# Layer 0's attention with its scores, exponentials and reciprocals one unit further ahead of the transposes, on four score buffers in place of three

## The chip, the cores and the metric

One core of one Trainium2 chip. The metric is the device time of one launch in microseconds, median of several executions. TensorE (PE) multiplies and transposes, VectorE (DVE) and ScalarE (ACT) read its results out of PSUM, GpSimd (POOL) works on SBUF only, and SyncE starts most of the loads. Each engine works through its own queue in order; semaphores order them against each other.

## The reference, cut to what matters

Four attention layers in a row, each with its projections and its MLP or norm. The change touches layer 0 alone, whose attention is

```python
# x: context (4, 64, 256); latents: (4, 256, 256); NH = 16 heads of DH = 16
h = jnp.concatenate([x, latents], axis=1)
q = (latents @ q_w + q_b).reshape(b, k_len, NH, DH)
kv = (h @ kv_w + kv_b).reshape(b, p + k_len, NH, DH, 2)
kmat, v = (kv[..., 0], kv[..., 1])
attn = jnp.einsum('bkhd,bnhd->bhkn', q, kmat) / DH
attn = jnp.where(full_mask[:, None, None, :], attn, -jnp.inf)
attn = jax.nn.softmax(attn.astype(jnp.float32), axis=-1).astype(q.dtype)
attn_out = jnp.einsum('bhkn,bnhd->bkhd', attn, v)  # then out_w, out_b, residual, rmsnorm, MLP
```

So for each of 4 batches and 16 heads there are 256 queries against 320 keys (256 latents, 64 of the context, the latter masked).

## The kernel before, in words

Layer 0's attention is cut into 64 units, 16 for each batch. A unit is one block of 128 queries and one pair of heads (`units0`, L299), so two score matrices of 128 x 320. Each unit passes through these stations:

- TensorE makes the scores (`scores0`, L568, matmul at L577) into a wide PSUM slot. Of three wide slots, two (`SCORES`) are for scores and one (`TURNS`) for transposes. A slot is taken again when it has been drained (`Ring`, `take_wide`); the scores of unit u therefore wait for the exponentials of unit u-2.
- VectorE (`front0`, L1277) adds the mask to 64 of the columns (L1282), takes the maxima (L1286) and multiplies them by -1/16 (L1287).
- ScalarE (`exp0`, L964) takes the exponentials out of PSUM into the SBUF tile `scoresb`, one instruction for each head with its row sum in `sums` (L970).
- VectorE (`middle0`, L1289) takes the reciprocal of the sums (L1291).
- GpSimd (`normalize0`, L1507) multiplies by it into `probs`, in two instructions (L1514) of 128x512 and 128x128. `probs` has two buffers, so it first waits until TensorE has turned unit u-2.
- TensorE (`turn_probs`, L474) transposes `probs` in five 128x128 pieces (L479) into the one wide slot for transposes.
- ScalarE (`probs_turned`, L937, copy at L897) copies them to SBUF, which frees that slot.
- After each fourth unit TensorE multiplies four transposed units with the values (`values0`, L581, L599).

The order in each queue is written out by hand as a loop over steps; step s is the one in which unit s is transposed. TensorE's step s is: transposes of unit s, scores of unit s+3, the value products if s is a multiple of 4, then one side product. ScalarE's is: the copy of the side product of step s-1, the copy of the transposes of s, the exponentials of s+2. VectorE's is: `front0` of s+2, `middle0` of s+1, its share of the side copy of step s-1, and at some steps more. GpSimd's step s is: the multiply of unit s, then a bias addition (steps 4 to 19).

The side products (`SIDE0`, `side_product0`) are the projections of queries, keys and values for the next batch, their placement into operands for the score products (`qhot` L554, `kpair` L564), and the output projection of the batch before (`proj`, L512). They share one narrow PSUM slot with their copies. The last batch has none of the next batch's. The side products of batch 0 are made ahead of the loop: `START0[0]` before the first scores, `START0[1]` at step -1, before that step's scores.

Two more things hang on the steps. At two steps of each later batch (18 and 19 of batch 1 and so on, `done0`) VectorE makes the statistics of a row block, GpSimd raises them to the power -1/2 (L1478) at the end of its step, and VectorE scales. At steps 22 and 38 VectorE splits weights of the MLP (`weights_low`, L224: a subtraction with both inputs in SBUF), and ScalarE copies them at steps 20 and 36 (L218).

The rings of `scoresb`, `mx`, `sums` and `rcp` have three buffers, taken by u % 3. `exp0` waits until GpSimd has multiplied unit u-3 out of its buffer.

Of the kernel before, what the change touches and what calls it, by code (L numbers as in the profile page):

```python
# [20 lines left out]
P = 128  # L21
B, S, D, T = 4, 256, 256, 64
# [7 lines left out]
KEYS0 = S + T  # L30
# [7 lines left out]
ALU = mybir.AluOpType  # L38
# [68 lines left out]
def build(nc, t, out):  # L107
    ctx = ExitStack()
    with ctx:
# [219 lines left out]
        def side0(step):  # L329
# [8 lines left out]
                return (job, b) if 0 < b < B else (None, None)  # L338
            return (job, b + 1) if b + 1 < B else (None, None)

        TURNED0 = 6

        def turned_probs(u):
# [31 lines left out]
        def _(pe):  # L375
# [229 lines left out]
            for job in START0[0]:  # L605
                side_product0(job, 0, (0, 1))
            n0 = len(units0)
            for step in range(-3, n0 + 3):
                if step == -1:
                    for job in START0[1]:  # L610
                        side_product0(job, 0, (0, 1))
                if 0 <= step < n0:
                    turn_probs(step)
                if step + 3 < n0:
                    scores0(step + 3)
                if step > 0 and step % 4 == 0:
# [273 lines left out]
        def _(act):  # L890
# [73 lines left out]
            def exp0(u):  # L964
                key = ("S", u)
                act.wait_ge(max_ready, u + 1)
                if u >= 3:
                    act.wait_ge(prob_ready, probcount[u - 2])
                for i in range(2):
                    nc.scalar.activation(scoresb[:, u % 3, i * KEYS0:(i + 1) * KEYS0],  # L970
                                         wide_ps[:, wide.slot(key), i * 512:i * 512 + KEYS0], ACT.Exp,
                                         scale=1.0 / 16, bias=mx[:, u % 3, i:i + 1],
                                         accum_out=sums[:, u % 3, i:i + 1]).then_inc(wide.drained[wide.slot(key)], 1)

            def exp(u, n):
                if n == 1024:
# [25 lines left out]
            for job in START0[0]:  # L1002
                side0_copy(job, 0)
            n0 = len(units0)
            for step in range(-2, n0 + 2):
                if step == 0:
                    for job in START0[1]:
                        side0_copy(job, 0)
                job, b = side0(step - 1)
                if job:  # L1010
                    side0_copy(job, b)
                if step - 2 >= 0 and (step - 2) % 8 == 7:
                    b, c = (step - 2) // 16, (step - 2) // 8 % 2
# [110 lines left out]
        def _(dve):  # L1124
# [152 lines left out]
            def front0(u):  # L1277
                b, r, q = units0[u]
                key = ("S", u)
                dve.wait_ge(*wide.full(key))  # L1280
                ps = wide_ps[:, wide.slot(key), :].rearrange("p (i n) -> p i n", i=2)
                link(v.tensor_tensor(ps[:, :, S:KEYS0], ps[:, :, S:KEYS0],  # L1282
                                     mask0[:, b, :].unsqueeze(1).broadcast_to([P, 2, T]), ALU.add))
                if u >= 3:
                    dve.wait_ge(*wide.empty(("S", u - 3)))
                link(v.tensor_reduce(mx[:, u % 3, 4:6], ps[:, :, 0:KEYS0], AX, ALU.max))  # L1286
                v.tensor_scalar(mx[:, u % 3, 0:2], mx[:, u % 3, 4:6], -1.0 / 16, None, ALU.mult).then_inc(max_ready, 1)  # L1287

            def middle0(u):  # L1289
                dve.wait_ge(*wide.empty(("S", u)))  # L1290
                v.reciprocal(rcp[:, u % 3, 0:2], sums[:, u % 3, 0:2]).then_inc(rcp_ready, 1)  # L1291

            dve.wait_ge(load["cols"], 16)
            for job in START0[0]:
# [1 line left out]
            dve.wait_ge(load["mask0"], 16)  # L1296
            link(v.tensor_scalar(mask0[:].rearrange("p b k -> p (b k)"), mask0i, 0, NEG0, ALU.is_equal, ALU.mult))
            n0 = len(units0)
            for step in range(-2, n0 + 5):
                if step == 0:  # L1300
                    for job in START0[1]:
                        side0_copy(job, 0)
                if step + 2 < n0:
                    front0(step + 2)
                if 0 <= step + 1 < n0:
                    middle0(step + 1)
                job, b = side0(step - 1)
                if job:
                    side0_copy(job, b)
# [146 lines left out]
        def _(pool):  # L1456
# [50 lines left out]
            def normalize0(u):  # L1507
                pool.wait_ge(rcp_ready, u + 1)
                if u >= 2:
                    pool.wait_ge(*wide.full(("T", u - 2)))  # L1510
                s3 = scoresb[:, u % 3, 0:2 * KEYS0].rearrange("p (i k) -> p i k", i=2)
                for lo, hi, o in ((0, S, 0), (S, KEYS0, 2 * S)):
                    n = hi - lo
                    g.tensor_tensor(probs[:, u % 2, o:o + 2 * n].rearrange("p (i k) -> p i k", i=2), s3[:, :, lo:hi],  # L1514
                                    rcp[:, u % 3, 0:2].unsqueeze(2).broadcast_to([P, 2, n]), ALU.mult).then_inc(prob_ready, 1)

            def spread_keys(layer, kbd, mask, heads_):
                pool.wait_ge(*wide.empty(("k", layer)))
# [102 lines left out]
```

## Time and profile before

| what | value |
|---|---|
| median of 3 runs | 840.12 us (840.08 to 841.82) |
| the profiled execution's own time | 840.74 us |
| its span, first to last instruction | 839.0 us |
| instructions | 12837 |
| busy: TensorE, VectorE, ScalarE, GpSimd | 730.8, 532.9, 403.9, 360.2 us |
| mean granted TensorE clock | 0.937 |
| first and last transposes of layer 0 | 25.70 and 199.30 us |

The profile lists each instruction with its start and length in microseconds from the start of the span. "x5" says how many instructions a line merges; the bracket at its end gives the idle time of the engine before it and the instruction whose completion ended that. A clock of 1.00 is TensorE's full 2.4 GHz, 0.50 the lower level of 1.2 GHz.

### The profile page before, as it was taken

What the parts mean: (1) busy time and instruction counts of PE and PEld (TensorE: products, weight loads), DVE (VectorE), ACT (ScalarE), POOL (GpSimd) and SP (SyncE); (2) the same over time, 40 slices, a digit from 0 to 9 for tenths busy, and PEclk for the clock granted to TensorE, in tenths of its full rate; (3) what the DMA queues carried; (4) which work ended last, traced back from release to release, by engine and by line L of the source; (5) the groups of instructions that cost most, each with busy time, mean ns of one, the idle gap of its engine ahead of it and who ended that gap; (6) DMA issues with size and microseconds to landing.
All of it is one profiled execution on the core that took longest, in us unless ns stands there. A gap on an engine that the chain in (4) does not pass through costs nothing.

```text
span 839.0 us, 12837 instructions
## 1 busy us (share of the span) xinstructions
PE 730.8 (87%) x4752; PEld 556.6 (66%) x4752; DVE 532.9 (64%) x1034; ACT 403.9 (48%) x965; POOL 360.2 (43%) x383
## 2 busy tenths in 40 slices
PE   8888888876399888779999999999998799776798
PEld 6676666654289445557875787876677688344598
DVE  6577776753844599955537674433888557398644
ACT  3687878854231377645652233653242131376421
POOL 2487554543700488844315561000765502177200
PEclk9899999967699999989999999999999899996899
DMA  8200000000000600002432000332000000200000
GB/s 318 95 1 1 2 1 2 2 1 2 0 1 1 201 1 2 1 1 92 161 103 98 1 1 1 101 104 97 1 0 1 1 1 1 100 1 1 1 20 32
DMA packets 24957, 32.51 MB, mean 39 GB/s; under 512 B 2752, under 2 KB 19392, under 8 KB 24768
## 3 DMA queue, kind: packets, MB, share of 16 engines
q1 hardware_dynamic: 24336, 31.10, 10.9%
q8 instruction: 39, 0.64, 0.3%
q10 hardware_dynamic: 560, 0.59, 0.2%
q14 instruction: 22, 0.18, 0.1%
HBM read 30.64 MB, written 1.05 MB: 38 GB/s over the span
## 4 chain that ended last, share of the span: by engine, by line
PE 62%; DVE 18%; POOL 8%; issue 7%; ACT 4%; DMA 1%; SPq 0%; POOLq 0%; DVEq 0%
PE wide_ps L432 9%; PE narrow_ps L451 8%; PE wide_ps L741 7%; PE wide_ps L692 6%; PE wide_ps L479 5%; PE narrow_ps L776 5%; POOL probs L1514 4%; PE wide_ps L715 4%; PE wide_ps L728 4%; DVE scoresb L1207 2%; DVE mx L1216 2%; PE narrow_ps L599 2%; DVE sums L1223 2%; PE wide_ps L412 2%; POOL probs L1500 2%
## 5 line engine op out<-in xcount | busy, mean ns | idle before, releaser
L479 PE MATMUL wide_ps<-ident,probs 128*128 128x128 f32 x640 | 96.3, 291 | 49.0 <-POOL probs L1500 23.1
L1492 POOL TENSOR_TENSOR scoresb<-scoresb,mx 128x768 f32<-128x768 f32 (+1 forms) x40 | 70.7, 1767 | 153.0 <-DVE mx L1214 115.4
L479 PEld LDWEIGHTS wide_ps<-ident,probs 128*128 128x128 f32 x640 | 77.2, 150 | 79.2 <-issue 63.2
L1514 POOL TENSOR_TENSOR probs<-scoresb,rcp 128x512 f32<-128x512 f32 (+1 forms) x128 | 89.4, 720 | 71.3 <-DVE rcp L1291 70.1
L897 ACT ACTIVATE probsT<-wide_ps 128x1024 f32<-128x1024 f32 (+1 forms) x73 | 64.3, 881 | 114.9 <-PE wide_ps L479 114.7
L1478 POOL TENSOR_TENSOR rstd<-veps,mhalf 128x1 f32<-128x1 f32 x56 | 32.0, 572 | 136.1 <-DVE veps L1142 136.1
L1500 POOL TENSOR_TENSOR probs<-scoresb,rcp 128x1024 f32<-128x1024 f32 x40 | 78.2, 1954 | 7.6 <-DVE rcp L1224 7.6
L432 PE MATMUL wide_ps<-xq_r,wstream_r 128*128 128x512 f32 x192 | 65.3, 424 | 8.7 <-issue 6.9
L451 PEld LDWEIGHTS narrow_ps<-wstream_r,hidden 128*128 128x128 f32 x576 | 69.2, 188 | 1.2 <-DVE xB L1170 0.5
L451 PE MATMUL narrow_ps<-wstream_r,hidden 128*128 128x256 f32 x576 | 69.7, 281 | 0.3 <-DVE xB L1170 0.3
L970 ACT ACTIVATE scoresb<-wide_ps,mx 128x320 f32<-128x320 f32 x128 | 66.4, 531 | 1.9 <-DVE mx L1287 1.6
L692 PE MATMUL wide_ps<-scoresb_r,probs_r 128*128 128x256 f32 x256 | 57.1, 306 | 4.8 <-DVE vwb L1370 4.2
L933 ACT ACTIVATE scoresb<-wide_ps,col 128x512 f32<-128x512 f32 x48 | 30.4, 685 | 63.0 <-PE wide_ps L432 63.0
L776 PE MATMUL narrow_ps<-region,probsT 128*128 128x256 f32 x256 | 58.0, 380 | 1.4 <-DVE xB L1170 1.4
L741 PE MATMUL wide_ps<-region,actT 128*128 128x512 f32 x128 | 59.0, 602 | 0.0
L1286 DVE TENSOR_REDUCE mx<-wide_ps 128x2 f32<-128x640 f32 x64 | 52.8, 824 | 2.3
L1323 DVE TENSOR_TENSOR wstream_r<-wstream,probs_r 128x256 fp32r<-128x256 f32 x64 | 26.7, 462 | 41.1 <-ACT probs_r L1059 41.1
L776 PEld LDWEIGHTS narrow_ps<-region,probsT 128*128 128x128 f32 x256 | 47.8, 191 | 7.5 <-DVE xB L1170 1.6
L692 PEld LDWEIGHTS wide_ps<-scoresb_r,probs_r 128*128 128x128 f32 x256 | 43.2, 196 | 12.4 <-issue 6.8
L432 PEld LDWEIGHTS wide_ps<-xq_r,wstream_r 128*128 128x128 f32 x192 | 38.9, 206 | 18.9 <-issue 7.5
L432 PE MATMUL wide_ps<-actT_r,wstream_r 128*128 128x512 f32 x96 | 41.1, 428 | 11.0 <-DVE actT_r L1184 11.0
L1170 DVE TENSOR_TENSOR xB<-narrow_ps,xB 128x256 f32<-128x256 f32 x48 | 20.2, 420 | 46.0 <-PE narrow_ps L451 24.1
(163 smaller groups left out, 1625.5 us busy)
## 6 DMA issues: line engine op xcount, KB each, us to landing
wstream<-in_L_xattn_wk SPq DMA_DIRECT2D x8, 512.0 KB, 4.0
wstream<-in_L_xattn_wv SPq DMA_DIRECT2D x8, 512.0 KB, 5.2
wstream<-in_L_xattn_wo SPq DMA_DIRECT2D x8, 512.0 KB, 6.4
wstream<-in_wqT SPq DMA_DIRECT2D x8, 512.0 KB, 7.5
wstream<-in_L_xattn_mlp_w SPq DMA_DIRECT2D x2, 1024.0 KB, 10.7
wstream<-in_L_xattn_w_fc SPq DMA_DIRECT2D x2, 1024.0 KB, 6.2
rows<-in_rows SPq DMA_DIRECT2D x1, 1280.0 KB, 14.0
xq<-in_x SPq DMA_DIRECT2D x1, 1024.0 KB, 11.8
```

The costliest lines, as they stand in the source:

```text
L432: m = mm(ps[:, j * 512:(j + 1) * 512], w1[pw][:, kc, f * P:(f + 1) * P], xparts[px][:, kc, half * 512:(half + 1) * 512], start=kc == 0 and ...
L451: m = mm(ps[:, 0:D], hidden[:, ph, f, qoff((q + i) % 4)], w2[pw][:, f, :], start=f == 0 and part == 0, stop=f == NF - 1 and part == 2)
L479: m = nc.tensor.transpose(ps[:, j * P:(j + 1) * P], probs[:, u % 2, j * P:(j + 1) * P], ident[:])
L692: last = mm(ps[:, m * 256:(m + 1) * 256], w[:, m, kc, :], cparts[:, part, kc, :], start=kc == 0 and i == 0, stop=kc == NC - 1 and i == 2)
L741: m = mm(ps[:, g * 512:(g + 1) * 512], actT[:, c, qoff(q)], G[:, c, 8 * g:8 * g + 8, b * T:(b + 1) * T], start=c == 0, stop=c == NC - 1)
L776: mm(ps[:, 0:D], probsT[:, u % 2, r * P:(r + 1) * P], VW[:, q // 2, r, :], start=r == 0, stop=False)
L897: nc.scalar.activation(dst, src, ACT.Identity, **kw).then_inc(ring.drained[ring.slot(key)], 1)
L970: nc.scalar.activation(scoresb[:, u % 3, i * KEYS0:(i + 1) * KEYS0], wide_ps[:, wide.slot(key), i * 512:i * 512 + KEYS0], ACT.Exp, scale=1 ...
L1286: link(v.tensor_reduce(mx[:, u % 3, 4:6], ps[:, :, 0:KEYS0], AX, ALU.max))
L1492: g.tensor_tensor(s3[:, first:], s3[:, first:], mx[:, u % 3, first:].unsqueeze(2).broadcast_to([P, 16 - first, n_scores]), ALU.subtract).t ...
L1500: g.tensor_tensor(probs[:, u % 2, :].rearrange("p (h k) -> p h k", h=16), s3[:, :, 0:T], rcp[:, u % 3, :].unsqueeze(2).broadcast_to([P, 16 ...
L1514: g.tensor_tensor(probs[:, u % 2, o:o + 2 * n].rearrange("p (i k) -> p i k", i=2), s3[:, :, lo:hi], rcp[:, u % 3, 0:2].unsqueeze(2).broadc ...
```

## The change

The loops of layer 0 begin one step earlier, and TensorE's scores, VectorE's `front0` and `middle0` and ScalarE's `exp0` stand one unit further ahead of the step. The multiply, the transposes, their copy, the values and all side work keep their step. The four rings of small and large buffers have four places. They lie in the same tiles, which are addressed flat: a unit's scores take 640 of the 3120 columns of `scoresb`, its maxima, sums and reciprocals 8 of 48 columns.

```diff
+        RING0, AHEAD0 = 4, 3
+
+        def scores_of(u):
+
+            return scoresb[:].rearrange("p a n -> p (a n)")[:, u % RING0 * 2 * KEYS0:(u % RING0 + 1) * 2 * KEYS0]
+
+        def pair_of(tile, u, o=0):
+
+            o += u % RING0 * 8
+            return tile[:].rearrange("p a n -> p (a n)")[:, o:o + 2]
...
-            for step in range(-3, n0 + 3):
+            for step in range(-1 - AHEAD0, n0 + 3):
                 if step == -1:
                     for job in START0[1]:
                         side_product0(job, 0, (0, 1))
                 if 0 <= step < n0:
                     turn_probs(step)
-                if step + 3 < n0:
-                    scores0(step + 3)
+                if step + 1 + AHEAD0 < n0:
+                    scores0(step + 1 + AHEAD0)
...
                 act.wait_ge(max_ready, u + 1)
-                if u >= 3:
-                    act.wait_ge(prob_ready, probcount[u - 2])
+                if u >= RING0:
+                    act.wait_ge(prob_ready, probcount[u - RING0 + 1])
...
-            for step in range(-2, n0 + 2):
+            for step in range(-AHEAD0, n0 + 2):
...
-                if step + 2 < n0:
-                    exp0(step + 2)
+                if step + AHEAD0 < n0:
+                    exp0(step + AHEAD0)
...
-                if u >= 3:
-                    dve.wait_ge(*wide.empty(("S", u - 3)))
+                if u >= RING0:
+                    dve.wait_ge(*wide.empty(("S", u - RING0)))
...
-            for step in range(-2, n0 + 5):
+            for step in range(-AHEAD0, n0 + 5):
                 if step == 0:
                     for job in START0[1]:
                         side0_copy(job, 0)
-                if step + 2 < n0:
-                    front0(step + 2)
-                if 0 <= step + 1 < n0:
-                    middle0(step + 1)
+                if step + AHEAD0 < n0:
+                    front0(step + AHEAD0)
+                if 0 <= step + AHEAD0 - 1 < n0:
+                    middle0(step + AHEAD0 - 1)
```

Every `[:, u % 3, ...]` of `exp0`, `front0`, `middle0` and `normalize0` becomes `scores_of(u)` or `pair_of(tile, u)`.

## Rows read from the trace of the kernel before

**Rows 1.** Busy time in the last batch: window, length, engines, PEclk, DMA share, GB/s

```profile
158.61:200.04 41.43, 28.84 (x276) 21.84 (x276) 22.86 (x68) 26.64 (x78) 21.98 (x32) 0.84 0.00 1
```

**Rows 2.** Waits from 25 to 206 us: total, times, longest

```profile
PE wide_ps L479 <- POOL probs L1514: 21.8, 20, 2.6
```

**Rows 3.** Timeline from 186 to 191 us: start, length, engine, line

```profile
187.13 0.70 ACT L897 ACTIVATE turned<-wide_ps 128x640 f32<-128x640 f32 x1 [0.23 <-PE wide_ps L479]
...
187.73 0.52 ACT L970 ACTIVATE scoresb<-wide_ps,mx 128x320 f32<-128x320 f32 x1
...
188.64 0.21 ACT L970 ACTIVATION_READ_ACCUMULATOR scoresb<-wide_ps,mx 128x1 f32 x1
188.74 0.71 ACT L897 ACTIVATE turned<-wide_ps 128x640 f32<-128x640 f32 x1
...
189.13 1.40 POOL L1514 TENSOR_TENSOR probs<-scoresb,rcp 128x512 f32<-128x512 f32 x2 [2.13 <-DVE rcp L1291]
...
189.84 0.82 DVE L1286 TENSOR_REDUCE mx<-wide_ps 128x2 f32<-128x640 f32 x1
```

**Rows 4.** TensorE's timeline of the last batch, its transposes alone

```profile
177.26 0.77 PE L479 MATMUL wide_ps<-ident,probs 128*128 128x128 f32 x5 [0.50 <-ACT turned L897]
...
180.04 1.30 PE L479 MATMUL wide_ps<-ident,probs 128*128 128x128 f32 x5 [1.21 <-POOL probs L1514]
...
186.28 0.81 PE L479 MATMUL wide_ps<-ident,probs 128*128 128x128 f32 x5
...
190.67 0.74 PE L479 MATMUL wide_ps<-ident,probs 128*128 128x128 f32 x5 [1.21 <-POOL probs L1514]
...
192.55 0.74 PE L479 MATMUL wide_ps<-ident,probs 128*128 128x128 f32 x5 [0.85 <-POOL probs L1514]
...
194.99 0.74 PE L479 MATMUL wide_ps<-ident,probs 128*128 128x128 f32 x5
...
199.30 0.74 PE L479 MATMUL wide_ps<-ident,probs 128*128 128x128 f32 x5 [1.70 <-POOL probs L1514]
```

**Rows 5.** Timeline around a row norm in the last batch

```profile
165.59 0.55 POOL L1478 TENSOR_TENSOR rstd<-veps,mhalf 128x1 f32<-128x1 f32 x1 [2.65 <-DVE veps L1142]
...
167.64 0.74 PE L479 MATMUL wide_ps<-ident,probs 128*128 128x128 f32 x5 [2.07 <-POOL probs L1514]
```

**Rows 6.** The chain that ended last, two value groups: start, length, what

```profile
59.39 1.23 PE narrow_ps L599 x40
...
184.06 2.29 PE narrow_ps L599 x40
```

**Rows 7.** Busy time from 180 to 187 us, columns as in rows 1

```profile
180.00:187.00 7.00, 6.69 (x60) 5.39 (x61) 2.98 (x11) 3.92 (x11) 4.19 (x6) 0.54 0.01 2
```

**Rows 8.** A dense stretch: busy time as in rows 1, and one wait of TensorE

```profile
81.00:119.00 38.00, 32.89 (x337) 26.84 (x336) 27.06 (x72) 33.47 (x90) 19.29 (x28) 1.00 0.01 2
...
93.04 0.74 PE L479 MATMUL wide_ps<-ident,probs 128*128 128x128 f32 x5 [0.23 <-POOL probs L1514]
```

**Rows 9.** The start: timeline of TensorE and ScalarE from 12 to 37 us

```profile
14.81 1.90 PE L535 MATMUL narrow_ps<-wstream,actT 128*128 128x256 f32 x8
...
17.22 0.20 ACT L970 ACTIVATION_READ_ACCUMULATOR scoresb<-wide_ps,mx 128x1 f32 x1
...
25.70 0.71 PE L479 MATMUL wide_ps<-ident,probs 128*128 128x128 f32 x5
...
33.46 1.30 PE L479 MATMUL wide_ps<-ident,probs 128*128 128x128 f32 x5 [0.91 <-POOL probs L1514]
```

**Rows 10.** Scaling of maxima (min/median/max ns, and one of them), transposes and a weight split

```profile
L1287 DVE TENSOR_SCALAR mx<-mx x64: 169/170/566, 16.1 to 195.0; 128x2 f32<-128x2 f32 x64
...
166.61 0.56 DVE L1287 TENSOR_SCALAR mx<-mx 128x2 f32<-128x2 f32 x1
...
87.21 0.71 PE L479 MATMUL wide_ps<-ident,probs 128*128 128x128 f32 x5
...
88.86 1.22 DVE L224 TENSOR_TENSOR wstream_r<-wstream,wstream_r 128x1024 fp32r<-128x1024 f32 x1
```

More of the change, by code:

```diff
@@ L966, in exp0 @@
                 act.wait_ge(max_ready, u + 1)
-                if u >= 3:
-                    act.wait_ge(prob_ready, probcount[u - 2])
+                if u >= RING0:
+                    act.wait_ge(prob_ready, probcount[u - RING0 + 1])
                 for i in range(2):
-                    nc.scalar.activation(scoresb[:, u % 3, i * KEYS0:(i + 1) * KEYS0],
+                    nc.scalar.activation(scores_of(u)[:, i * KEYS0:(i + 1) * KEYS0],
                                          wide_ps[:, wide.slot(key), i * 512:i * 512 + KEYS0], ACT.Exp,
-                                         scale=1.0 / 16, bias=mx[:, u % 3, i:i + 1],
-                                         accum_out=sums[:, u % 3, i:i + 1]).then_inc(wide.drained[wide.slot(key)], 1)
+                                         scale=1.0 / 16, bias=pair_of(mx, u)[:, i:i + 1],
+                                         accum_out=pair_of(sums, u)[:, i:i + 1]).then_inc(wide.drained[wide.slot(key)], 1)
             def exp(u, n):
@@ L1283, in front0 @@
                                      mask0[:, b, :].unsqueeze(1).broadcast_to([P, 2, T]), ALU.add))
-                if u >= 3:
-                    dve.wait_ge(*wide.empty(("S", u - 3)))
-                link(v.tensor_reduce(mx[:, u % 3, 4:6], ps[:, :, 0:KEYS0], AX, ALU.max))
-                v.tensor_scalar(mx[:, u % 3, 0:2], mx[:, u % 3, 4:6], -1.0 / 16, None, ALU.mult).then_inc(max_ready, 1)
+                if u >= RING0:
+                    dve.wait_ge(*wide.empty(("S", u - RING0)))
+                link(v.tensor_reduce(pair_of(mx, u, 4), ps[:, :, 0:KEYS0], AX, ALU.max))
+                v.tensor_scalar(pair_of(mx, u), pair_of(mx, u, 4), -1.0 / 16, None, ALU.mult).then_inc(max_ready, 1)
             def middle0(u):
                 dve.wait_ge(*wide.empty(("S", u)))
-                v.reciprocal(rcp[:, u % 3, 0:2], sums[:, u % 3, 0:2]).then_inc(rcp_ready, 1)
+                v.reciprocal(pair_of(rcp, u), pair_of(sums, u)).then_inc(rcp_ready, 1)
             dve.wait_ge(load["cols"], 16)
@@ L1510, in normalize0 @@
                     pool.wait_ge(*wide.full(("T", u - 2)))
-                s3 = scoresb[:, u % 3, 0:2 * KEYS0].rearrange("p (i k) -> p i k", i=2)
+                s3 = scores_of(u).rearrange("p (i k) -> p i k", i=2)
                 for lo, hi, o in ((0, S, 0), (S, KEYS0, 2 * S)):
@@ L1514, in normalize0 @@
                     g.tensor_tensor(probs[:, u % 2, o:o + 2 * n].rearrange("p (i k) -> p i k", i=2), s3[:, :, lo:hi],
-                                    rcp[:, u % 3, 0:2].unsqueeze(2).broadcast_to([P, 2, n]), ALU.mult).then_inc(prob_ready, 1)
+                                    pair_of(rcp, u).unsqueeze(2).broadcast_to([P, 2, n]), ALU.mult).then_inc(prob_ready, 1)
             def spread_keys(layer, kbd, mask, heads_):
```

## The prediction, made before the changed kernel was run

> **What bounds layer 0 now.** I began with the busy time by batch. The last of the four batches (units 48 to 63) has almost no side products left and still takes 41.43 us, while no engine is busy in it for more than 28.84 [rows 1]. So it waits. The totals of waits say for what: 20 times in layer 0 a group of transposes found TensorE idle until GpSimd's multiply was done, 21.8 us together [rows 2].
>
> Then one ring, followed event by event in the last batch. The transposes of unit 57 begin at 186.28 [rows 4]. ScalarE copies them at 187.13, its next exponentials (unit 59) end at 188.64 + 0.21 = 188.85, VectorE's reciprocal releases GpSimd, which multiplies from 189.13 for 1.40 [rows 3], and TensorE turns unit 59 at 190.67 [rows 4]. The ring spans two units because exponentials run two ahead: 190.67 - 186.28 = 4.39, or 2.19 us a unit. Nothing faster is open while the multiply is in it.
>
> **Which rings the change opens.** Counted by the step of the transposes, nothing but the multiply moves. Before, at step s, ScalarE exponentiates unit s+2, VectorE reduces s+2 and inverts s+1; after, s+3, s+3 and s+2. TensorE makes scores s+3 before and s+4 after, into the same two score slots, so they still wait for exponentials made one step earlier. Side copies, row statistics and weight splits keep their step. Only this differs: the reciprocal at VectorE's step s now serves the transposes of s+2 instead of s+1. The ring above then holds three units, 4.39 / 3 = 1.46 a unit, and is no longer the longest.
>
> Late next are two rings. ScalarE alone: copy at 187.13, next copy at 188.74, 1.61 a unit [rows 3]. The two score slots: exponentials end at 188.85, the maximum behind them runs 189.84 + 0.82 = 190.66, its scaling about 0.2, exponentials 188.85 - 187.73 = 1.12: 192.0, or 3.13 for two units, 1.57 each [rows 3]. I take 1.65, the 1.61 with a few hundredths lost between the two.
>
> **The last batch.** Up to unit 54 I change nothing: the transposes at 167.64 waited 2.07 us for a multiply that stood in GpSimd's queue behind a row-norm power, which waited for statistics that VectorE makes at the same step as before [rows 5]. From unit 54 to 63 the turns run from 177.26 to 199.30, 22.04 us for nine steps [rows 4]. Two of them also carry the value products (after units 56 and 60). Seven plain steps: 7 x 1.65 = 11.55. The value step with scores took 194.99 - 192.55 = 2.44 at full clock [rows 4]; the second has no scores left in it, about 0.5 less, 1.9; ScalarE's copy of attended values adds some 0.2 to each. 2.44 + 1.9 + 0.4 = 4.74. Sum 16.3, so **5.7 us saved**. This counts both value groups at full clock. Before, the one at 184.06 took 2.29 us against 1.23 for the same 40 matmuls at 59.39 [rows 6], because the granted clock averaged 0.54 of full (nearly all at the lower level, 1.2 GHz) from 180 to 187 [rows 7], right after TensorE sat idle for 1.21 before 180.04 [rows 4]. That idle time goes, so I take the full clock; at the lower level 1.06 less is saved.
>
> **The dense batches.** From 81 to 119 ScalarE is busy 33.47 of 38.00 us; most waits for the multiply are hidden under its queue there. What shows is a wait of 0.23 at the transposes of unit 24 [rows 8], with a fellow in each neighbouring batch: 3 x 0.23 = **0.7 saved**. The bound above is all of ScalarE's idle time, 4.5 here and some 13.6 in the three dense stretches; the bound below is nothing. I stay near the bottom because side products and their copies keep their step and end the other waits.
>
> **The lead-in, which pays.** Scores of unit 2 are now made before the opening side products, and their slot is free only when unit 0's exponentials end, 17.22 + 0.20 = 17.42; the side products started at 14.81 [rows 9]. TensorE's in-order queue holds all of the opening products behind that wait: with some 0.3 for the two score products, 2.9 late, and so the first transposes, 28.6 for 25.70 [rows 9]. VectorE reduces unit 2 ahead of its opening copies, but those wait for the late products anyway. Then it is won back, for unit 1's multiply is already done at 28.6. Following the slots (0.7 copy, 1.12 exponentials, 1.4 mask to maximum, 1.4 multiply) I get transposes of units 0 to 3 at 28.6, 30.2, 32.2 and 33.9, the last where 33.46 stood [rows 9]. **0.4 lost**; between 0 and 2.9.
>
> **GpSimd against VectorE.** The 2-element scaling of maxima takes 0.17 in the median and up to 0.57; one of 0.56 began at 166.61, during the first half (1.05 long) of the multiply that followed the power at 165.59, and ended with it [rows 5, 10]. So two such instructions exclude one another. The multiply of unit u, early now, waits for the transposes of unit u-2: unit 24's starts at 87.21 + 0.71 = 87.92 and runs to 89.3, across the weight split that VectorE starts at 88.86 [rows 10]; unit 40's meets the second split likewise. No row shows a split held, so I bound it: 0 to 1.4 each (the pair's length); 0.5 taken, the 0.44 of that overlap being the nearest, **1.0 lost** in two. Elsewhere the scaling has slack before ScalarE needs its result.
>
> The Trainium skill (SBUF — State Buffer, Who interferes with whom) states a rule: a VectorE instruction with two SBUF inputs and a GpSimd instruction that reads SBUF exclude each other for the whole instruction. By it the splits are held some 0.4 and 0.9, 1.3 where I took 1.0; no row here shows a split held.
>
> The addressing edits (a ring of four in the same tiles) change no shape or count: the same instructions, no DMA moved, SyncE untouched. The work after unit 63 and the later layers shift whole.
>
> **Sum.** -5.7 - 0.7 + 0.4 + 1.0 = -5.0. The profiled execution took 840.74 (span 839.0), so 835.7 by it; the median of the runs is 0.62 lower, 840.12, so **835.1**. A measurement can tell about 0.2%, 1.7 us, from no change.
>
> **Rivals.**
> (a) The lower clock stays in the last batch: one group of values 1.06 longer, two transposes 0.5 together: 836.7. For it: from 167 to 173 TensorE still idles behind row norms. 0.15.
> (b) The dense batches gain too: two fifths of the 13.6 idle comes back, 5.5 more, 829.6. Against: ScalarE's queue is nearly full, and what it waits for there are side products. 0.12.
> (c) Two score slots set the pace, and running ahead gives only storage; lead-in and splits alone count, 840.1 + 1.4 = 841.5, or 840 where they are hidden. Against it: their ring of 1.57 is shorter than 2.19. 0.08.
> (d) Slower: the multiply, held until the transposes two back, slides over VectorE's scaling in every unit and holds maxima, exponentials and side copies by 0.57 - 0.17 = 0.40. It decides from 5.0 + 1.7 = 6.7 lost, 17 units on the path; with 23 of the 64 the time is 844.3. For it: the rows of the scaling. Against: few units have VectorE on the path. 0.05.
> The forecast has 0.60.
>
> **Range and chances.** Low end: (b), 829.5. High end: (a) with 1.2 lost in the lead-in and 2.0 in the splits, 838.5, rounded up to 839.0. Faster by over 0.2%: forecast, (a) and (b), 0.87; within: (c), 0.08; slower: (d), 0.05.
>
> **What would show it.** Turns of units 54 to 63 near 1.65 apart where 2.19 stood; the multiply hardly named among the waits of transposes, but for the row norms, whose 2 us waits stay; first transposes near 28.6; the value groups of the last batch near 1.23; the two splits over 1.22. Wrong would be: scaling rows of 0.5 all over with ScalarE waiting on VectorE, or last turns still over 2 us apart while each multiply ended long before.

## The result and the profile after

| | before | after |
|---|---|---|
| median of the runs in this comparison | 840.45 us (4 runs, 840.08 to 841.82) | 828.71 us (4 runs, 827.73 to 831.71) |
| the profiled execution, its span | 840.74, 839.0 us | 827.73, 826.0 us |
| mean granted TensorE clock | 0.937 | 0.957 |
| first and last transposes of layer 0 | 25.70, 199.30 us | 28.53, 193.69 us |

The ratio is 0.9863, interval 0.9836 to 0.9891: 11.7 us less, where 5.0 was forecast, and 828.7 lies just under the low end of the range, 829.5. The profiled execution after is the fastest of its four, so the two profiles lie 13.0 apart. A kernel is now and then executed in a slower state with a lower clock; one run below was (840.49, experiment 2), and its ratio leaves it out. Lines of the kernel after are those of before plus 11 (transposes L490, their copy L908, exponentials L981, scaling of maxima L1298, multiply L1525, scores L588).

The page of the kernel after: its busy times, and the transposes (busy time and mean ns of one, then the idle time before them; all four layers).

```profile
PE 719.2 (87%) x4752; PEld 544.8 (66%) x4752; DVE 537.8 (65%) x1034; ACT 403.6 (49%) x965; POOL 362.3 (44%) x383
...
L490 PE MATMUL wide_ps<-ident,probs 128*128 128x128 f32 x640 | 93.4, 285 | 39.1 <-POOL probs L1511 24.0
```

The same 4752 matmuls are busy for 11.6 us less than before (730.8): already a sign of the clock, since the change takes none away.

The totals of waits from 25 to 200 us, and a transposition behind a row norm in the last batch, kernel after.

```profile
PE wide_ps L490 <- POOL probs L1525: 9.2, 5, 2.1
```

```profile
168.87 0.94 PE L490 MATMUL wide_ps<-ident,probs 128*128 128x128 f32 x5 [2.08 <-POOL probs L1525]
```

Twenty waits for the multiply, 21.8 us [rows 2], have become five. All five stand at or behind row norms; the first behind each norm is as long as it was, 2.08 beside 2.07 [rows 5].

The timeline of the kernel after in the last batch: transposes of units 54, 56, 57 and 63, and some events behind unit 58's.

```profile
177.90 0.77 PE L490 MATMUL wide_ps<-ident,probs 128*128 128x128 f32 x5 [0.50 <-ACT turned L908]
...
181.13 0.77 PE L490 MATMUL wide_ps<-ident,probs 128*128 128x128 f32 x5
...
183.87 0.76 PE L490 MATMUL wide_ps<-ident,probs 128*128 128x128 f32 x5
...
186.27 0.71 ACT L908 ACTIVATE turned<-wide_ps 128x640 f32<-128x640 f32 x1
...
186.44 0.56 PE L588 MATMUL wide_ps<-kpair,qhot 128*128 128x320 f32 x2 [0.25 <-ACT scoresb L981]
...
186.66 1.40 POOL L1525 TENSOR_TENSOR probs<-scoresb,rcp 128x512 f32<-128x512 f32 x2 [0.49 <-DVE rcp L1302]
...
187.86 0.73 ACT L908 ACTIVATE turned<-wide_ps 128x640 f32<-128x640 f32 x1
...
193.69 0.77 PE L490 MATMUL wide_ps<-ident,probs 128*128 128x128 f32 x5 [0.80 <-ACT probsT L908]
```

Plain steps (those without value products) are 1.55 to 1.62 long, ScalarE's two copies stand 1.59 apart without idle time between them, and TensorE's waits now name ScalarE. Units 54 to 63 take 193.69 - 177.90 = 15.79 for 22.04 [rows 4].

**Where the 13.0 us between the two profiles came from.** Stages are cut at the starts of instructions, the same ones in each kernel; this table, worked out from those starts, is used for the experiments too.

| stage, from the end of the one before up to | before | after |
|---|---|---|
| last transposes of layer 0 | 199.30 | 193.69 |
| "exit": first projection of the last batch (before L512) | 4.58 | 3.55 |
| "entry": first low product of the MLP (L432 with `actT_r`) | 23.92 | 21.72 |
| first scores of layer 1 | 57.15 | 58.03 |
| "preparation": first head product of layer 2 (L715) | 91.95 | 89.94 |
| first scores of layer 2 (L741) | 62.10 | 62.19 |
| last head product | 137.35 | 135.68 |
| last scores of layer 2 | 48.67 | 48.67 |
| "last stretch": last product of the last MLP (L451) | 211.17 | 209.70 |

In this pair layer 0 gave 5.6, the exit 1.0, the entry 2.2, preparation 2.0, the head products 1.7, the last stretch 1.5, and 1.0 went back in between. So over half of the gain lies behind unit 63, in code that is the same in both.

How far a single pair can be trusted, the profiles of the experiments tell. Layer 0 of before is in two of them (199.30, and 195.42 in experiment 6), that of after in five (190.86 to 193.69, experiments 5, 8, 9 and 10 among them), so its share is 5 us in the mean, and 5.6 is one draw. Behind unit 63 up to the last product, before and experiments 1 and 6 (less its delay) took 636.9 to 639.6, after and experiments 2 and 4 took 629.5 to 632.3: 6.7 in the mean for the 7.4 of this pair. Exit and entry repeat to 0.05 us wherever nothing in them was edited. The head products (135.7 to 138.3) and the last stretch (208.1 to 213.8) do not, and no experiment here ties their 1.7 and 1.5 to the change.

Busy time by windows at the exit and in the preparation (its ends rounded), of before and then of after (columns as in rows 1: length, PE, PEld, DVE, ACT, POOL, granted clock).

```profile
199.30:203.88 4.58, 3.10 (x45) 2.31 (x46) 0.00 (x0) 1.18 (x2) 0.00 (x0) 0.58 0.02 4
285.00:376.90 91.90, 72.42 (x515) 43.59 (x514) 77.95 (x146) 57.04 (x183) 62.55 (x46) 0.93 0.03 11
```

```profile
193.69:197.24 3.55, 2.07 (x46) 1.59 (x46) 0.00 (x0) 1.18 (x2) 0.00 (x0) 1.00 0.02 5
277.00:366.90 89.90, 69.70 (x514) 41.60 (x514) 77.84 (x146) 57.19 (x183) 61.42 (x45) 0.96 0.04 12
```

The counts match but for one instruction here and there, VectorE's and ScalarE's busy times within 0.3%; TensorE's time and its clock differ. At the exit the clock is 0.58 against 1.00, and all of the 1.03 us is TensorE's: 3.10 busy against 2.07.

The timeline from the projections to the first low product, of before and then of after.

```profile
203.88 2.05 PE L512 MATMUL narrow_ps<-wstream,xq 128*128 128x256 f32 x4 [0.69 <-ACT xq L897]
...
208.32 2.88 PE L494 MATMUL wide_ps<-ctxT,wkrep 128*128 128x256 f32 x8
...
212.15 14.51 POOL L1520 TENSOR_TENSOR region<-headbuf,head 128x4096 f32<-128x4096 f32 x2 [1.42 <-ACT headbuf L897]
...
213.40 6.35 DVE L1182 CAST xq_r<-actT 128x1024 fp32r<-128x1024 f32 x1 [2.28 <-ACT actT L897]
...
219.79 7.96 DVE L1184 TENSOR_TENSOR actT_r<-actT,xq_r 128x1024 fp32r<-128x1024 f32 x1
...
227.80 0.80 PE L432 MATMUL wide_ps<-actT_r,wstream_r 128*128 128x512 f32 x1 [6.75 <-DVE actT_r L1184]
```

```profile
197.24 1.10 PE L523 MATMUL narrow_ps<-wstream,xq 128*128 128x256 f32 x4 [0.69 <-ACT xq L908]
...
199.82 1.89 PE L505 MATMUL wide_ps<-ctxT,wkrep 128*128 128x256 f32 x8
...
202.99 14.11 POOL L1531 TENSOR_TENSOR region<-headbuf,head 128x4096 f32<-128x4096 f32 x2
...
203.06 7.13 DVE L1159 TENSOR_SCALAR xn<-xB,rstd 128x256 f32<-128x256 f32 x1 [0.66 <-POOL rstd L1489]
...
210.11 7.54 DVE L1193 CAST xq_r<-actT 128x1024 fp32r<-128x1024 f32 x1
...
218.96 0.80 PE L443 MATMUL wide_ps<-actT_r,wstream_r 128*128 128x512 f32 x1
```

Read it by GpSimd. It spreads layer 1's keys (`spread_keys`) in two instructions of some 7 us, as soon as ScalarE has copied the keys out of PSUM, and VectorE's work on the MLP's input stands still meanwhile. In both kernels the first low product follows the start of the spreading by nearly the same time: 227.80 - 212.15 = 15.65 and 218.96 - 202.99 = 15.97. Spreading begins 8.27 us behind the first projection before, and 5.75 after, since projections and keys run at the full clock, 1.10 for 2.05 and 1.89 for 2.88. That is the 2.2 of the entry.

### The profile page after: what moved, and what is told of

Same layout as the page of the kernel before. It is cut to its first block, busy times and chain, and to the rows that moved or that the text cites. A ratio compares the mean times of both kernels' runs of the same rounds, so it can differ in the third digit from the quotient of the medians.

```text
span 826.0 us, 12835 instructions
## 1 busy us (share of the span) xinstructions
PE 719.2 (87%) x4752; PEld 544.8 (66%) x4752; DVE 537.8 (65%) x1034; ACT 403.6 (49%) x965; POOL 362.3 (44%) x383
## 4 chain that ended last, share of the span: by engine, by line
PE 62%; DVE 17%; ACT 8%; issue 6%; POOL 6%; DMA 1%; SPq 0%; DVEq 0%; POOLq 0%
PE wide_ps L443 9%; PE narrow_ps L462 8%; PE wide_ps L752 7%; PE wide_ps L703 5%; PE narrow_ps L787 5%; PE wide_ps L490 4%; PE wide_ps L739 4%; PE wide_ps L726 3%; ACT scoresb L981 3%; DVE scoresb L1218 2%; PE narrow_ps L610 2%; DVE mx L1227 2%; POOL probs L1511 2%; DVE sums L1234 2%; PE wide_ps L423 2%
## 5 line engine op out<-in xcount | busy, mean ns | idle before, releaser
L490 PE MATMUL wide_ps<-ident,probs 128*128 128x128 f32 x640 | 93.4, 285 | 39.1 <-POOL probs L1511 24.0
L490 PEld LDWEIGHTS wide_ps<-ident,probs 128*128 128x128 f32 x640 | 74.2, 146 | 68.1 <-issue 58.4
L908 ACT ACTIVATE probsT<-wide_ps 128x1024 f32<-128x1024 f32 (+1 forms) x73 | 64.5, 883 | 110.6 <-PE wide_ps L490 110.2
L1525 POOL TENSOR_TENSOR probs<-scoresb,rcp 128x512 f32<-128x512 f32 (+1 forms) x128 | 91.5, 738 | 56.9 <-DVE rcp L1302 29.4
L981 ACT ACTIVATE scoresb<-wide_ps,mx 128x320 f32<-128x320 f32 x128 | 66.8, 537 | 3.8 <-DVE mx L1298 3.5
L703 PE MATMUL wide_ps<-scoresb_r,probs_r 128*128 128x256 f32 x256 | 54.7, 297 | 5.3 <-DVE vwb L1381 4.2
L703 PEld LDWEIGHTS wide_ps<-scoresb_r,probs_r 128*128 128x128 f32 x256 | 41.4, 188 | 13.1 <-issue 7.5
```

Of the source, the lines that this page charges most:

```text
L490: m = nc.tensor.transpose(ps[:, j * P:(j + 1) * P], probs[:, u % 2, j * P:(j + 1) * P], ident[:])
L703: last = mm(ps[:, m * 256:(m + 1) * 256], w[:, m, kc, :], cparts[:, part, kc, :], start=kc == 0 and i == 0, stop=kc == NC - 1 and i == 2)
L908: nc.scalar.activation(dst, src, ACT.Identity, **kw).then_inc(ring.drained[ring.slot(key)], 1)
L981: nc.scalar.activation(scores_of(u)[:, i * KEYS0:(i + 1) * KEYS0], wide_ps[:, wide.slot(key), i * 512:i * 512 + KEYS0], ACT.Exp, scale=1.0 ...
```

## Theories

**T1**, the forecast's: distance takes the multiply out of the ring (the cycle of events that spans two units), and everything behind unit 63 shifts whole; storage alone does nothing. **T2**: buffers give the gain. **T3**, formed on the table above: TensorE waits less at the end of layer 0, so its clock stays up through the exit, and what follows is shortened by that. **T3'**, rival to it: what follows depends on when it comes, not on the clock.

## Experiments

Ratios are against runs of the kernel before on the same chip (its median there 840.2 to 840.3), so medians of different experiments can be set beside one another to about a microsecond. A stage's length is from one profiled execution.

**1. Four buffers, old distance** (kernel after with one line changed).

```diff
-        RING0, AHEAD0 = 4, 3
+        RING0, AHEAD0 = 4, 2
```

> The changed kernel with its four buffers, but scores, maxima, exponentials and reciprocals back at their old distance (two units ahead). Theory 'ring': all of the gain comes from taking the multiply out of the two-unit ring, so buffers alone give nothing: 840.4, last transposes of layer 0 near 199.3 us. Theory 'buffers': the fourth buffer relieves a wait of its own (the exponentials' for the multiply three units back): then under 838.

837.63 us, ratio 0.9976 (0.9956 to 0.9995). The profiled execution was the slowest of ten, 841.48. Its transposes of units 59 and 60:

```profile
188.68 0.74 PE L490 MATMUL wide_ps<-ident,probs 128*128 128x128 f32 x5 [1.21 <-POOL probs L1525]
190.56 0.74 PE L490 MATMUL wide_ps<-ident,probs 128*128 128x128 f32 x5 [0.84 <-POOL probs L1525]
```

The old waits, 1.21 and 0.84 where 1.21 and 0.85 stood [rows 4]; units 54 to 63 take 21.44, 0.6 less than before. 837.63 is just under the 838 that was named as the sign of T2, so T1's "storage alone does nothing" isn't exact either: a quarter of a per cent comes from the buffers, and the rest of the gain doesn't.

**2. Three buffers, new distance.**

```diff
-        RING0, AHEAD0 = 4, 3
+        RING0, AHEAD0 = 3, 3
```

> The changed kernel with three buffers again and the distance of three units kept. Exponentials of unit s+3 stand behind the copy of the transposes of unit s, which already needs unit s multiplied, so theory 'ring' says that the third buffer is free in time and the fourth not needed: 828.7, within 1.5. Theory 'buffers': the exponentials wait for the multiply and the time goes back towards 835 to 840.

830.22 us over all four runs, 828.28 in the profiled one, 0.9877 (0.9836 to 0.9919); units 54 to 63 take 15.78. The distance is the change; at that distance the fourth buffer can't be told from no fourth buffer.

**3. Four ahead.**

```diff
-        RING0, AHEAD0 = 4, 3
+        RING0, AHEAD0 = 4, 4
```

> The changed kernel with the distance raised once more, to four units. The ring through the multiply is then 4.3 / 4 = 1.1 us a unit; at three units (1.46) it was already shorter than ScalarE's own 1.61. Theory 'ring': the pace of the last batch stays at 1.55 to 1.62 a unit and the extra scores ahead of the opening products cost one more microsecond or so of lead-in: turns of units 54 to 63 spaced as with the change, total 828 to 830.5. If the pace were still set by the distance, the last batch shrinks again: under 826.

833.93 us, 0.9922 (0.99 to 0.9944), over the 828 to 830.5 expected. Plain steps stay at 1.56 to 1.62: with the multiply out of the ring, more distance finds nothing. The two value steps are longer, 3.30 and 2.17, so units 54 to 63 take 16.60. And it costs a second wait ahead of the opening products (TensorE's timeline):

```profile
17.35 0.56 PE L588 MATMUL wide_ps<-kpair,qhot 128*128 128x320 f32 x2 [2.48 <-ACT scoresb L981]
18.61 0.90 PE L588 MATMUL wide_ps<-kpair,qhot 128*128 128x320 f32 x2 [0.71 <-ACT scoresb L981]
19.31 3.13 PE L546 MATMUL narrow_ps<-wstream,actT 128*128 128x256 f32 x8
```

The opening products, 1.90 long before [rows 9], take 3.13 here, and unit 0 is turned at 31.25 (28.53 after), unit 4 at 42.36 (36.66). Preparation, 92.9 for 89.9, adds to the loss.

**4. Opening products ahead of the third unit's scores** (kernel after; the same edit in ScalarE's and VectorE's loops, from step 0 to -1).

```diff
-                if step == -1:
+                if step == -2:
                     for job in START0[1]:
                         side_product0(job, 0, (0, 1))
```

> The changed kernel with the opening side products (START0[1]) and their copies one step earlier on TensorE, ScalarE and VectorE, so ahead of the scores of unit 2. The prediction's lead-in step says that the first transposes come back from 28.5 to about 25.7, and that most of this is given back at once, because unit 1 is then inverted behind the opening copies: transposes of unit 4 at 36.0 to 36.7 (36.66 with the change), total 828 to 829. The rival, that the late start is carried through, says 825.9.

827.28 us, 0.9846 (0.9815 to 0.9876), against 828.71 no certain difference, and between the 828 to 829 expected and the 825.9 of the rival. Unit 0 is turned at 26.80 for 28.53, but unit 4 at 36.23 for 36.66: of the 1.7 gained at unit 0, 0.4 is left four units on, since the kernel after wins most of its late start back by itself. Between unit 0 and unit 4 it takes 8.1 us in each of the five profiles with this layer 0, where this kernel takes 9.4. The 25.70 of before isn't reached: the third unit's scores stand behind the opening products, ahead of unit 0's transposes.

**5. A delay at the exit.** Eight linked copies of the identity (each waits for the one before it) into a tile of their own on ScalarE, ahead of the last copy of attended values; extra work, never read. In the kernel after:

```diff
+                    if step - 2 == n0 - 1:
+                        for i in range(8):
+                            nc.scalar.copy(idle[:], ident[:].unsqueeze(1).broadcast_to([P, 2, P])).then_inc(idled, 1)
+                            act.wait_ge(idled, i + 1)
```

> The changed kernel with eight idle copies (128x256, linked one behind the other) on ScalarE ahead of the last copy of attended values of layer 0, some 3 us between layer 0's attention and everything behind it. Theory 'rigid' (the later layers' time doesn't depend on when they start): 828.7 + 3.0 to 3.5, that is 831.7 to 832.2. Theory 'phase' (the extra gain after layer 0 is where the low clock level happens to fall): another amount by over 1.5 us, most likely up, 834 to 837.

835.69 us, 0.996 (0.9933 to 0.9987). A delay of 3.48 cost 7.0 by the medians, 8.1 by the ratios. The timeline of that kernel:

```profile
194.00 3.46 ACT L1031 COPY idle<-ident 128x256 f32<-128x256 f32 x8 [1.42 <-PE narrow_ps L612]
...
198.10 2.05 PE L525 MATMUL narrow_ps<-wstream,xq 128*128 128x256 f32 x4 [4.17 <-ACT xq L910]
...
202.54 2.79 PE L507 MATMUL wide_ps<-ctxT,wkrep 128*128 128x256 f32 x8
...
221.92 0.79 PE L445 MATMUL wide_ps<-actT_r,wstream_r 128*128 128x512 f32 x1 [6.75 <-DVE actT_r L1201]
```

After 4.17 us without work TensorE's projection takes 2.05 again and the keys 2.79, and the stages are those of before: entry 23.82, then 57.11, preparation 92.0. From the last transposes to the first head product of layer 2 it is 179.92 against 173.23: 6.7 of the 7.0, of which the delay itself is half.

**6. The same delay in the kernel before.**

> The kernel before with the same eight idle copies on ScalarE ahead of the last attended values (3.5 us in the run with the change). Theory 'phase in two modes': after layer 0 the changed kernel runs its exit and the layer 2 preparation in a quick mode (exit from projection to first MLP product 21.7 us, preparation 89.9) and the kernel before, and the changed one when delayed, in a slow mode (23.8 and 92.0). The kernel before is in the slow mode already, so a delay costs only itself: 840.2 + 3.5 = 843.7, stages 23.8 and 92.0. Theory 'each shift is a new draw': 840 to 847, with other stage lengths.

844.63 us, 1.0051 (1.0031 to 1.007): 4.4 for 3.5. Its profiled execution was the fastest of ten, 840.42, with exit 4.58 + 3.48 = 8.06, and entry 23.94, then 57.16 and preparation 91.9, unchanged. There the delay had nothing more to spoil. This speaks for T3. Its profile also gives a warning: its layer 0, the very instructions of before, ended at 195.42 instead of 199.30. Much of the 3.9 us is the clock: it is 0.92 against 1.00 from 60 to 81 us, and unit 41 is turned 4.55 behind unit 40 in the one (the clock 0.76 from 138 to 145), 2.95 in the other. Differences of up to 4 us in layer 0 between two single profiles prove nothing.

**7. TensorE kept busy in the kernel before.** Four transposes of the identity into unused columns of PSUM ahead of the transposes of units 55, 59, 62 and 63 (while TensorE waits for the multiply), ahead of the last group of values and of the first projection of the last batch; extra work, never read.

```diff
+            def keep_warm(ps, o):
+                for i in range(4):
+                    nc.tensor.transpose(ps[:, o:o + P], ident[:], ident[:])
...
+                if u in (55, 59, 62, 63):
+                    keep_warm(ps, 768)
```

> The kernel before, with 24 transposes of the identity (results never read) put into TensorE's waits for the multiply at units 55, 59, 62 and 63 and into its two waits of layer 0's exit. They fill idle time, so by themselves they cost nothing. If the changed kernel's gain behind unit 63 comes from TensorE being at full clock there, this one gets it without the change: value group of units 52 to 55 at 1.23 in place of 2.29, last transposes near 198 (199.3 less 1.1), exit 3.55 + 21.7 in place of 4.58 + 23.9, preparation 89.9, total 833.5 to 835. If the gain comes from something else: 838 to 841.

835.87 us, 0.9935 (0.9912 to 0.9958), a little over the 833.5 to 835 expected. TensorE's windows and its timeline in that kernel:

```profile
180.00:187.00 7.00, 4.82 (x64) 3.69 (x64) 4.84 (x14) 6.35 (x18) 4.50 (x7) 1.00 0.01 2
196.11:199.66 3.55, 3.10 (x54) 2.45 (x54) 0.00 (x0) 1.18 (x2) 0.00 (x0) 1.00 0.02 5
279.20:372.00 92.80, 73.84 (x514) 44.25 (x513) 78.04 (x146) 57.04 (x183) 62.54 (x46) 0.91 0.04 12
```

```profile
198.90 0.66 PE L386 MATMUL narrow_ps<-ident 128*128 128x128 f32 x4
199.66 1.10 PE L520 MATMUL narrow_ps<-wstream,xq 128*128 128x256 f32 x4
...
202.24 1.89 PE L500 MATMUL wide_ps<-ctxT,wkrep 128*128 128x256 f32 x8
```

The clock from 180 to 187 is 1.00 for 0.54 [rows 7], the exit 3.55 and the entry 21.71, the very lengths of the kernel after, with nothing of layer 0's distance changed: extra matmuls put into waits took 4.4 us off, of which units 54 to 63 are 2.2 (19.82 for 22.04). So exit and entry are shown to hang on the clock, in both directions: 4.58 and 23.9 in all profiles with the old distance and no extra transposes (before, experiments 1 and 6, less the delay), 3.55 in all with the new and no delay, and 21.7 wherever the spreading of keys was left alone too. The preparation took 92.8, not 89.9: T3 does not reach that far by itself.

**8. Spreading held until VectorE has the normed rows** (kernel after, GpSimd).

```diff
+            pool.wait_ge(xn_ready, NQ)
             spread_keys(1, kbd1, head8, 16)
```

> The changed kernel with GpSimd's spreading of layer 1's keys (two instructions of 7.05 us) waiting for the last row norm. In both traces the first MLP product that needs a split input starts 15.65 to 16.0 us behind the start of the spreading, because VectorE's casts and subtractions stand still during it. If the spreading holds VectorE, the last norm (7.13 us in the changed kernel, 0.35 before) takes 0.35 again, the spreading starts about 0.5 later, and the product too: nothing gained, 829 to 829.5. If the 7.13 us of the norm were on the path by themselves, the product comes 6.8 us earlier: 822.

831.37 us, 0.9866 (0.9827 to 0.9905), where 829 to 829.5 was expected if nothing is gained and 822 if the norm counted; entry 21.89. The norm's 7.13 is gone, and the next two instructions of VectorE take 7.16 and 7.96 in its place: who is held doesn't matter, that someone is held for the length of the spreading does.

**9. Spreading held until the MLP's input is split.**

```diff
+            pool.wait_ge(x_split, 4)
             spread_keys(1, kbd1, head8, 16)
```

> The changed kernel with the spreading waiting until VectorE has split the MLP's input. If the spreading holds VectorE, the norm, casts and subtractions take 0.35, 0.69 and 1.23 again and the first low product starts near 206.5 instead of 218.96; the two 7 us blocks then fall into the MLP, where VectorE splits the hidden layer each 2.8 us and TensorE stalls for part of them: total 820 to 826. If VectorE's long instructions are long for another reason, nothing changes: 828.7.

826.81 us, 0.9858 (0.9801 to 0.9915), over the 820 to 826 expected; one of its four runs took 836.75, and there is no certain difference from 828.71. The first low product comes at 205.84, an entry of 8.69 for 21.72, but 8.3 is given back by layer 1's first scores (66.38 for 58.03), since the spreading now holds the weight splits and the casts of `hidden` (timeline):

```profile
207.57 9.23 DVE L224 TENSOR_TENSOR wstream_r<-wstream,wstream_r 128x1024 fp32r<-128x1024 f32 x2
207.73 15.98 POOL L1531 TENSOR_TENSOR region<-headbuf,head 128x4096 f32<-128x4096 f32 x2 [4.80 <-DVE actT_r L1195]
216.72 7.54 DVE L1207 CAST hidden<-scoresb 128x1024 fp32r<-128x1024 f32 x1
```

**10. The same, with the spreading cut into eight instructions**, one for each batch and half, in layers 1 and 3 alike; only layer 1's also waits for the split (TensorE's waits on `kbd_ready` are 8 and 16 for 2 and 4).

```diff
-                    g.tensor_tensor(kbd[:, c],
-                                    kT2[:, c, :].rearrange("p (b k) -> p b k", b=B).unsqueeze(2).broadcast_to([P, B, heads_, T]),
-                                    mask[:].unsqueeze(1).unsqueeze(3).broadcast_to([P, B, heads_, T]), ALU.mult
-                                    ).then_inc(kbd_ready, 1)
+                    for b in range(B):
+                        g.tensor_tensor(kbd[:, c, b], kT2[:, c, b * T:(b + 1) * T].unsqueeze(1).broadcast_to([P, heads_, T]),
+                                        mask[:].unsqueeze(2).broadcast_to([P, heads_, T]), ALU.mult).then_inc(kbd_ready, 1)
```

> As the run with the spreading behind the split, but the spreading in eight pieces of some 1.8 us (four batches by two channel halves) for each of layers 1 and 3, so that VectorE's splits get their turn between two pieces. In that run one cast of the hidden layer was held for 7.54 us and TensorE stood still for some 8 to 10 us behind it. If instructions exclude one another one at a time, no VectorE instruction is held longer than a piece and TensorE's long stall goes: 818 to 822. If VectorE is only let in when GpSimd's queue is empty, it is as before, 826.8.

820.32 us, 0.9765 (0.9725 to 0.9805), and no run over 820.56: 8.4 under the kernel after.

```profile
204.83 4.06 DVE L224 TENSOR_TENSOR wstream_r<-wstream,wstream_r 128x1024 fp32r<-128x1024 f32 x2
204.99 21.14 POOL L1532 TENSOR_TENSOR region<-headbuf,head 128x1024 f32<-128x1024 f32 x8 [4.80 <-DVE actT_r L1195]
208.81 2.39 DVE L1207 CAST hidden<-scoresb 128x1024 fp32r<-128x1024 f32 x1
```

GpSimd is at it for 21.14 in place of 15.98, and that costs nothing. VectorE gets in between two pieces: the splits take 4.06 for 9.23, a cast 2.39 for 7.54. Entry 8.70, and 63.65 up to layer 1's scores, together 7.4 less than in the kernel after (72.35 for 79.75): that is the gain of 8.4, but for what differs between single profiles. Against experiment 9 alone the pieces gain 6.5 in the medians, of which these two stages show 2.7; another 2.75 stands in layer 0, whose code is the same, so what the pieces are worth beside the later start is known only roughly.

**11. Both that, and the opening products first.**

> The pieces of the run above together with the opening side products first. If the two savings are independent, 1.4 us less than that run (828.7 less 827.3), that is 816.5 to 821.

818.97 us, 0.9751 (0.971 to 0.9793): the best version, 9.7 under the kernel after, though 1.4 under experiment 10 is within the intervals.

## Why the prediction was right and wrong

**The last batch, right.** Forecast 16.3 us for units 54 to 63, measured 15.79; saved 6.25 for 5.7. The ring of ScalarE's queue was read right (1.61 in [rows 3], 1.59 after). The step of the first value group took 183.87 - 181.13 = 2.74, the second 1.92, together 4.66 for the 4.74 of the sum; plain steps were 1.59 in the mean where I had allowed 1.65. Both value groups ran at the full clock, as assumed (1.00 from 180 to 187). Rival (a) falls by that clock, and (c) because units stand 1.59 apart and no longer 2.19. This part repeats: units 54 to 63 took 22.04 and 22.16 in the two profiles of the old layer 0, 15.78 to 15.79 in all five of the new.

**The lead-in, right.** Forecast 28.6, 30.2, 32.2 and 33.9, measured 28.53, 30.03, 31.91 and 33.52: 0.1 lost by unit 3, not 0.4. That the times agree to 0.1 is partly luck, since unit 0 was turned anywhere from 28.48 to 30.31 in profiles of the same layer 0, and before turned unit 4 at 36.14 in experiment 6, at 37.38 here; the spacing is what repeats, 5.0 from unit 0 to unit 3 in all five, where 5.3 was forecast.

**The splits, right in themselves.** The timeline of the kernel after, and one window:

```profile
87.34 2.38 POOL L1525 TENSOR_TENSOR probs<-scoresb,rcp 128x512 f32<-128x512 f32 x2 [1.40 <-PE wide_ps L490]
...
87.78 1.69 DVE L224 TENSOR_TENSOR wstream_r<-wstream,wstream_r 128x1024 fp32r<-128x1024 f32 x1
...
91.44 1.27 PE L575 MATMUL narrow_ps<-kparts,place 128*128 128x320 f32 x4 [1.87 <-DVE qhot L1271]
...
92.51 1.27 PE L490 MATMUL wide_ps<-ident,probs 128*128 128x128 f32 x5
```

```profile
92.00:97.00 5.00, 5.00 (x53) 4.16 (x52) 2.04 (x7) 2.32 (x6) 1.68 (x3) 0.50 0.00 0
```

The split is held: 1.69 for 1.22 [rows 10], 0.47 for the 0.5 taken, and the second one too (1.69 at 134.56). The multiply beside it takes 2.38 for 1.40. VectorE is then late with `qhot`, and TensorE waits 1.87 for it where before it waited 1.47; the row of before, and then the same one in experiment 10's kernel, whose layer 0 is that of after:

```profile
92.05 0.76 PE L564 MATMUL narrow_ps<-kparts,place 128*128 128x320 f32 x4 [1.47 <-DVE qhot L1260]
```

```profile
92.26 0.77 PE L575 MATMUL narrow_ps<-kparts,place 128*128 128x320 f32 x4 [1.87 <-DVE qhot L1271]
```

From 92 to 97 the clock of the kernel after is at the lower level where before it was full [rows 8], and unit 24, turned 0.53 earlier than before, is followed by unit 25 5.27 later, not 2.94: 2.3 lost in one place. But that isn't the price of the held split. In experiment 10's kernel the same split of 1.69 and the same wait of 1.87 were followed by the full clock (1.00 from 92 to 97), and unit 25 came 2.93 behind unit 24; and in experiment 7's, with the old distance, a split of 1.22 and a wait of 1.46, the clock fell (0.66) and it took 4.54. So the clock fell in some profiles of one and the same code and not in others; what decides isn't found. The held split itself costs the 0.4 by which the wait grew.

**The dense batches, read short.** The forecast counted one wait of 0.23 in each of three batches. Before has nine waits for the multiply there, three each of about 0.23, 0.48 and 0.55, 3.8 us in all, and after has none of them. Little of it was on the path: from unit 8 to 16 it takes 19.4 for 19.7, and from 28 to 32 9.0 for 9.2, in every profile of either layer 0. By unit 54 the kernel after is 0.64 behind, close to the net 0.7 of the forecast (0.4 and 1.0 lost, 0.7 gained), but that agreement is luck: unit 20 was 1.08 ahead, and of two profiles of the same layer 0 (after and experiment 10) one reaches unit 54 2.8 before the other.

**The step that failed:** "The work after unit 63 and the later layers shift whole." They didn't. Forecast 0, measured 7.4 in the profile (13.0 - 5.6), and this puts the result under the range. Of it exit and entry, 3.2, are shown: the clock level that TensorE leaves layer 0 with, by experiments 5 and 7, one taking it away and one giving it. The sum had looked at the clock from 180 to 187 [rows 7], and stopped there. The last transposes stood behind a wait of 1.70 for the multiply [rows 4]; that wait goes too, and the low clock that followed it in the values, the projections and the keys was never priced. The other 4.2 are not shown to come from the change.

**Still open: the preparation and the later stretches.** Preparation differs with the clock; the table rows are above. Time at the lower level, worked out as (1 - granted clock) x 2 x length, was 12.9 us in the preparation before and 7.2 after. These windows show where, the first two of before, the last two of after:

```profile
365.00:370.00 5.00, 3.80 (x25) 2.19 (x25) 3.17 (x10) 1.49 (x4) 0.66 (x1) 0.77 0.00 0
...
375.00:380.00 5.00, 5.00 (x29) 4.77 (x29) 1.91 (x3) 1.82 (x5) 4.76 (x7) 0.74 0.00 0
```

```profile
357.00:362.00 5.00, 3.47 (x31) 2.42 (x31) 3.92 (x12) 1.98 (x5) 0.66 (x1) 1.00 0.00 0
...
367.00:372.00 5.00, 5.00 (x35) 4.10 (x35) 3.26 (x5) 3.12 (x9) 4.77 (x7) 1.00 0.00 0
```

What sets it isn't found. Preparation was 89.4 to 90.4 in seven kernels (after and experiments 2, 4, 8 to 11), all with the fast exit and distance 3, and 91.9 to 92.0 in four with the slow exit; but experiment 7 (92.8) and experiment 3 (92.9) had the fast exit and a long preparation. So a fast exit isn't enough, and T3' may hold there: when the work arrives may decide too. The head products took 135.7 or 135.8 in three kernels (after, experiments 2 and 3) and 137.1 to 138.3 in the ten others, the last stretch 208.1 to 213.8 over all thirteen, without an order that I can see.

**The rivals.** (b), at 829.6, had the size nearly right and the place wrong: what the dense batches gained, 0.2 or 0.3 here and there, is lost again by unit 54. (d) didn't come: two-element scalings have a median of 0.17 as before, only their longest is now 0.75. ScalarE found its maxima late five times, 3.5 us in all, where it was twice and 1.6 before.

**VectorE and GpSimd.** The overlap that was priced at 0.5 a split in layer 0 cost up to 7 us an instruction right behind it, in both kernels, and had gone unseen; in the one after a scaling of 0.35 us took 7.13, a cast of 0.69 took 7.54. The Trainium skill (SBUF — State Buffer, Who interferes with whom) says that a VectorE scaling or cast which also uses the ports shared with GpSimd, or a VectorE instruction with two SBUF inputs, is blocked for the whole GpSimd instruction that came first; the trace agrees, 7.13 and 7.54 beside pieces of 7.05 (14.11 / 2), and experiment 10 shows the other half of it: between two instructions of GpSimd VectorE gets in.

## What to carry to other kernels

When software pipelining takes a stage out of a ring, count each ring by its events and divide it by its distance, and take the longest that is left: the multiply's fell to 1.46, ScalarE's queue at 1.61 was next, and 1.59 was measured. Then follow TensorE's clock past the end of the changed stage, to the next instruction that the rest waits for; a wait of a microsecond or two taken out just before a stage ends can be worth several behind it, and a few idle transposes in such waits show whether it is so. Take a stage's length from several profiles where you can: the clock behind one and the same wait was full in one execution and at the lower level in another. And look for long GpSimd instructions beside VectorE work: cut into pieces and started later they cost GpSimd 5 us more (21.14 for 15.98), and the kernel became 8.4 shorter.

## What the runs showed that I had not expected

- A delay of 3.5 us costs 7.0 behind a full clock and 4.4 behind a low one, by the medians (experiments 5 and 6).
- Twenty-four extra transposes in waits shorten a kernel by 4.4 us (experiment 7).
- The same layer 0, instruction for instruction, ended 3.9 us apart in two executions (195.42 and 199.30), and a wait of 1.87 us at one and the same place was followed by the full clock in one and by the lower level in another.
- One GpSimd instruction of 7 us stretches a VectorE scaling of 256 columns twentyfold, from 0.35 to 7.13 us.
